# Loading sorted edge slots: rows by tile turned on TensorE, or slots read straight into place

## The reference

```python
N_NODES, DIM_H, N_EDGES = 6250, 256, 100000
h = layernorm(x)
msg = silu(concat(h[src], h[dst], weight) @ mW1 + mb1)          # one row per edge
msg = silu(layer_norm(msg, ln_g, ln_b) @ mW2 + mb2)
agg = segment_sum(msg, src, num_segments=N_NODES)
x = x + h + silu(concat(h, agg) @ uW1 + ub1) @ uW2 + ub2
x = x + moe(layernorm(x))                                       # 8 experts, top 2, 256 wide, gelu
```

## Time and profile before

| | us |
|---|---|
| median of three runs | 2960.49 (2957.86 to 2960.51) |
| the profiled execution, its own time | 2958.22 |
| its span in the trace | 2956.3 |
| end of the scatters' issue (POOL) | 593.4 |
| issue of the seven loads (SP) | 594.54 to 597.73 |
| first instruction of `messages` | 605.50 |

### The profile page before, as it was taken

The page is one execution under the profiler, slowest core; times in us unless marked ns, Lnnn a source line. Parts: engine busy times, 40 slices in busy tenths (PEclk is TensorE's granted clock), DMA queues, the critical chain, the costliest instruction groups (busy, mean ns, idle before and its releaser), DMA issues. The chain is left out here.

```text
span 2956.3 us, 71061 instructions
## 1 busy us (share of the span) xinstructions
PE 2419.7 (82%) x17442; PEld 2248.8 (76%) x17443; DVE 2239.3 (76%) x6897; ACT 1846.8 (62%) x4147; POOL 1595.2 (54%) x2124
## 2 busy tenths in 40 slices
PE   0000666169999999999999999999979699999999
PEld 0000444159999999999999999999869599999999
DVE  9991444369999999999999999999946755555555
ACT  5430111048888888888888888888845555555554
POOL 0017777468878788787878878788725300000000
PEclk9999999669999999999999999999989899999999
DMA  4000233122222222222222222222343100000000
GB/s 146 0 2 9 80 86 87 41 71 73 74 71 73 70 74 71 72 73 71 72 73 71 73 71 73 72 72 73 68 120 94 31 11 10 10 10 10 10 10 14
DMA packets 110143, 169.39 MB, mean 57 GB/s; under 512 B 27420, under 2 KB 81822, under 8 KB 109961
## 3 DMA queue, kind: packets, MB, share of 16 engines
q0 software_dynamic: 48832, 112.23, 13.2%
q1 hardware_dynamic: 59156, 55.09, 6.2%
q10 hardware_dynamic: 2100, 1.45, 0.2%
HBM read 138.66 MB, written 29.79 MB: 57 GB/s over the span
## 5 line engine op out<-in xcount | busy, mean ns | idle before, releaser
L1006 POOL DMA_INDIRECT rows<-b_rows,dst_row x838 | 848.2, 1012 | 231.5 <-issue 146.7
L1133 PE MATMUL ps_z<-w_hi,t_hi 128*128 128x256 f32 x1676 | 547.0, 326 | 0.0
L1134 PE MATMUL ps_z<-w_lo,t_hi 128*128 128x256 f32 x1676 | 467.9, 279 | 0.0
L1135 PE MATMUL ps_z<-w_hi,t_lo 128*128 128x256 f32 x1676 | 467.5, 279 | 0.0
L1120 PE MATMUL ps_agg<-rows,onehot 128*126 128x256 f32 x1676 | 453.7, 393 | 16.7 <-DVE node_rows L1156 14.3
L1039 ACT ACTIVATE rows<-rows,shift,rstd_m 128x256 f32<-128x256 f32 x838 | 452.4, 587 | 0.0
L1156 DVE TENSOR_TENSOR node_rows<-node_rows,ps_agg 126x256 f32 x838 | 344.9, 412 | 101.7 <-issue 85.5
L438 POOL DMA_INDIRECT sorted_edges<-pay,place x245 | 238.1, 972 | 279.7 <-DVE place L776 199.3
L1066 ACT ACTIVATE rows<-rows 128x512 f32<-128x512 f32 x419 | 265.0, 633 | 185.4 <-DVE rows L1212 179.7
L1120 PEld LDWEIGHTS ps_agg<-rows,onehot 128*126 128x126 f32 x1676 | 281.3, 187 | 70.4 <-DVE node_rows L1156 20.1
L1782 DVE TENSOR_TENSOR g_lo<-g,g_hi 128x504 fp32r<-128x504 f32 x200 | 136.6, 683 | 253.8 <-ACT g_hi L1700 253.8
(11 more groups left out here) (274 smaller groups left out, 5991.6 us busy)
## 6 DMA issues: line engine op xcount, KB each, us to landing
rows<-b_rows,dst_row POOLq DMA_INDIRECT x838
b_rows<-b_out SPq DMA_DIRECT2D x50, 126.0 KB
u_rows<-u_out SPq DMA_DIRECT2D x50, 126.0 KB
xh_rows<-xh_out SPq DMA_DIRECT2D x50, 126.0 KB
u_row<-u_rows SPq DMA_DIRECT2D x50, 126.0 KB
xh_row<-xh_rows SPq DMA_DIRECT2D x50, 126.0 KB
node_rows<-in_x SPq DMA_DIRECT2D x1, 6174.0 KB
out_rows<-node_rows SPq DMA_DIRECT2D x49, 126.0 KB
```

What stands on the lines that cost most here:

```text
L1006: nc.gpsimd.indirect_dma_start(rows[r][:, i, :], None, dram["b_rows"], bass.IndirectOffsetOnAxis(ap=dst_row[:, r, i:i + 1], axis=0)).then_ ...
L1133: pe.matmul(z, t_hi[:, k, i, c, :], w2_hi[:, c, :], start=(c == 0), stop=False)
L1134: pe.matmul(z, t_hi[:, k, i, c, :], w2_lo[:, c, :], start=False, stop=False)
L1135: mm = pe.matmul(z, t_lo[:, k, i, c, :], w2_hi[:, c, :], start=False, stop=(c == KC - 1))
```

## The change

The loads of L399 read the same blocks of `sorted_edges`, but write `slots` directly: the DRAM side is viewed as "(t p) w -> p t w", so that partition p takes slot p of every tile, 16 bytes at each step of 2,048 bytes. There are still seven loads on SP with one semaphore each. `by_tile`, the 28 transposes on PE, the four copies on DVE and the three on ACT are gone, and with them their three semaphores.

```diff
-        by_tile = early_sb("by_tile", [P, BLOCKS, P * WORDS])
-        assert at[0] <= pay_at + 4 * PIECES * PIECE * WORDS
...
-        ps_s = [ps_n, ps_c]
...
-        by_tile_turned = sem("by_tile_turned")
-        slots_even = sem("slots_even")
-        slots_odd = sem("slots_odd")
...
             for b in range(BLOCKS):
                 n = min(P, TILES - b * P)
-                sp.dma_start(by_tile[0:n, b, :], dram["sorted_edges"][b * P * P:(b * P + n) * P, :]
-                             .rearrange("(t p) w -> t (p w)", p=P)).then_inc(by_tile_in[b], 16)
+                sp.dma_start(slots[:, b * P:b * P + n, :], dram["sorted_edges"][b * P * P:(b * P + n) * P, :]
+                             .rearrange("(t p) w -> p t w", p=P)).then_inc(by_tile_in[b], 16)
             for b in range(BLOCKS):
                 sp.wait_ge(by_tile_in[b], 16)
...
-            for b in range(1, BLOCKS, 2):
-                n = min(P, TILES - b * P)
-                act.wait_ge(by_tile_turned, b + 1)
-                nc.scalar.activation(slots[:, b * P:b * P + n, :],
-                                     ps_s[1][:].rearrange("p (w t) -> p t w", w=WORDS)[:, 0:n, :], ACT.Copy
-                                     ).then_inc(slots_odd, 1)
...
-            for b in range(BLOCKS):
-                n = min(P, TILES - b * P)
-                pe.wait_ge(by_tile_in[b], 16)
-                if b >= 2:
-
-                    pe.wait_ge(slots_odd if b % 2 else slots_even, b // 2)
-                words = by_tile[0:n, b, :].rearrange("t (p w) -> t p w", w=WORDS)
-                for w in range(WORDS):
-                    tr = pe.transpose(ps_s[b % 2][:, w * P:w * P + n], words[:, :, w], ident[0:n, 0:n])
-                tr.then_inc(by_tile_turned, 1)
...
-            for b in range(0, BLOCKS, 2):
-                n = min(P, TILES - b * P)
-                dve.wait_ge(by_tile_turned, b + 1)
-                nc.vector.tensor_copy(slots[:, b * P:b * P + n, :],
-                                      ps_s[0][:].rearrange("p (w t) -> p t w", w=WORDS)[:, 0:n, :]
-                                      ).then_inc(slots_even, 1)
```

## The result

| | before | after |
|---|---|---|
| median, us | 2960.50 (4 runs, 2957.86 to 2960.66) | 3014.91 (4 runs, 3014.20 to 3017.25) |
| the profiled execution, its own time / span | 2958.22 / 2956.3 | 3017.25 / 3015.3 |
| first issue of the seven loads | 594.54 | 594.14 |
| first instruction of `messages` | 605.50 | 659.61 |
| between the two | 10.96 | 65.47 |

A forecast was written before the change was run, and what follows sets the result against it. Bound: an uncovered serial stretch of 10.96 us before `messages`. New way 3.1 + 63.7 + 0.4 = 67.2 us, so 56.2 us more than the old, on 2960.5: forecast 3017 us (+1.9%), range 2990 to 3075.

The forecast's parts named there:

- Nothing covers the stretch: From first load issue at 594.54 to `messages` at 605.50 us: each us added or saved there is one of the whole.
- The gain is 2.6 us, not PE's 6.6: Removed transposes and copies: only 2.6 us, from 602.6 to 605.20, lay behind the loads, of 6.64 us PE work.
- A run costs an engine 9.5 ns, 63.7 us in all: New loads: 6,704 16-byte runs an engine, at 9.0 ns plus 0.5 for twelve more bytes, take 63.7 us.
- b1's 4-byte elements: Strided HBM loads in `route`, same queue: 2,096 packets in 18.9 us of one engine, 9.0 ns each, basis of the price.
- 3.1 and 0.4 us beside it: Beside the new transfer: 3.1 us for issue, start and completion, 0.4 us from landing to the first instruction of `messages`.
- The clock of PE costs nothing: PE at 0.50 through the turning and start of `messages`: priced 0, with up to 3.3 us either way kept in range.
- The dearer read: Rival: strided HBM reads of the new loads cost 15.6 ns a run, +97 us, 3058 us; chance 0.18.
- the estimate of 95 us of transfer: In the dearer-read rival: 19 times the old loads' 5.0 us, total 3048 us.
- The queue's issue as bound: Rival: SP's issue at up to 1.1 ns a run needs 118.7 us for the loads, +111 us, 3072; chance 0.08.
- Cheaper by a third: Rival: runs of the new loads cost 5.9 ns as in POOL's scatters, 39.6 us, +32 us, 2993; chance 0.09.
- not slower: Rival: short runs of the loads are joined and cost by bytes alone, -2.5 us, 2958; chance 0.04.
- What would show it: Profile signs: 107,000 more packets, DMA share near 1, 25 to 30 GB/s, end moving along; over 12 ns means dearer read.

## Why the prediction was right

By its own steps:

- **Nothing covers the stretch.** Held. The start of `messages` moved by 54.1 us and the median by 54.4.
- **The gain is 2.6 us, not PE's 6.6.** Held: 2.5 us, shown by the kernel with 2,048-byte runs.
- **A run costs an engine 9.5 ns, 63.7 us in all.** Measured 9.2 ns and 62 us. The 9.0 ns of b1's 4-byte elements was the right row, and 52 times as many runs an engine did not change it. The 0.5 ns for twelve bytes more was the wrong refinement: 8 and 16 bytes cost the same. It cost the forecast 2 of its 56.2 us. The reason behind the number is weaker than the number. 9.0 ns was the mean length of a packet's record and was taken for the time that an engine needs. In the long loads records are 13.0 ns long, the engines take a run in 5.8 ns at times, and the average pace is 9.2. That the short loads' record and the long loads' pace are the same number was not shown to be more than luck; that the pace is one price for each run, whatever it holds up to 64 bytes, was shown.
- **3.1 and 0.4 us beside it.** Held in sum: packets flowed for some 62 us of the 65.47. From the last landing to `messages` it is 0.8 us and not 0.4.
- **The clock of PE costs nothing.** PEclk was 0.50 through the stretch and rose to 1.00 some 33 us after the start of `messages`, before the change some 30. The medians show no cost, but the 2 to 3 us by which the rest of the program is longer in the kernels with 65 us or more of loading stay open, and the clock may have part in them.
- **The dearer read** fell twice: by the total, and by the kernel that reads in order and needs the same. For the estimate of 95 us of transfer, the 19-fold price of the Trainium skill (VectorE: DVE Perf Modes, The three transpose paths) was set against the old contiguous loads, which is not the path that the figure compares with; the strided loads took 62 us, 12 times the 5.0 of the old ones. As a warning of the direction it was right.
- **The queue's issue as bound** fell with two queues, which gained nothing. The durations of the issues alone would have spoken for it, since they add up to the whole transfer; but they doubled when two queues issued.
- **Cheaper by a third** and **not slower** fell with the count of packets, one to each run, and their price. The 5.9 ns of POOL's 64-byte rows is not the pace of this queue over a whole load, 8.9 to 9.7 ns at 64 bytes, though it comes close to its peaks.
- **What would show it.** The count and the rate came as said, and the end moved with the start of `messages` within the spread. The DMA share did not (1.46 in place of 1), and the sign set for the dearer read, a packet over 12 ns, came true by the records (13.0) although that rival is false: the sign rested on records, which overlap.

The 10.5 ns a packet of the Trainium skill (DMA: Bandwidth & Descriptors, Bandwidth) would have given 70.4 us of transfer by the prediction's estimate. The Trainium skill states it for loads issued from POOL; the measured 62 us decide for the trace's own row.

## What to carry to other kernels

Before a strided DMA takes the place of a contiguous one with a transpose behind it, count its runs. In loads over all 128 partitions like these, runs / 16 x 9.2 ns was the time, whatever a run held up to 64 bytes, and the work on PE that was saved was worth only what of it stood behind the last load (2.5 of 6.6 us). A price could be read here from the kernel's own trace, from small strided loads of a bias; take from such a place both the length of the records and the wall clock (9.0 and 15.6 ns), since neither is sure to be the pace of a long load. And look at the first us of a block in which everybody waits: a memset there cost 12 us that an idle engine could take earlier.

## What the runs showed of the hardware

- The average price of a run on this queue is flat from 8 to 64 bytes (8.9 to 9.7 ns), 9.6 to 11.3 at 128, 17.6 to 20.9 at 256 and 89 to 112 at 2,048; the two ends are for two fixed times beside the packets. At 128 and 256 bytes the rate is nearly the same, 200 and 218 GB/s.
- For up to a microsecond the 16 engines take a 16-byte run in 5.8 ns each (44 GB/s), and on average in 9.3 (27 GB/s). What holds the average down was not found.
- Loads of eight partitions peak at half that rate (22 GB/s) and cost 1.5 us of issue each.
- A DMA share above 1 (1.46): with small packets the records overlap, and the busy time of a packet (13.0 ns) is then above its price (9.3).
- While DVE cleared 12,800 elements a partition, an issue of POOL's indirect DMA took 12.29 us; without the clearing 0.96. That the one held up the other is shown by taking it away; through what was not tried. The Trainium skill (SBUF — State Buffer, SBUF: two separate sides) describes such a lock between DVE and the descriptors that POOL writes, for DVE's two-port modes, with a copy as its example; this trace shows a memset beside it, and whether that memset ran in such a mode was not tried.
